# Moving a value product of the context ahead of the second scores, and the second half's value products and sums side by side behind them

## The reference

```
x = x + tanh(g_xattn[0]) * L0_attention(layernorm(x), ctx, ctx)        # causal, 16 heads of 32
x = x + tanh(g_ffn[0])   * L0_ffn(layernorm(x), w_gate_up, w_proj)     # weights made ternary in groups of 64
x = x + tanh(g_xattn[1]) * L1_attention(layernorm(x), ctx, ...)        # projections, normed q and k, softmax, output projection
x = x + tanh(g_ffn[1])   * L1_ffn(layernorm(x), w_gv, w_out)           # ternary weights, 8-bit activations
```

## Time and profile before

| what | before |
|---|---|
| median of 3 runs | 1074.51 us (1073.95 to 1074.6) |
| the profiled execution's own time | 1073.95 us |
| its span, first to last instruction | 1072.2 us |
| TensorE busy | 1046.0 us, 98% |
| VectorE, ScalarE, GpSimd busy | 833.3, 585.6, 119.2 us |
| granted clock of TensorE, mean | 1.000 |
| the chain that ended last, by engine | TensorE 81%, VectorE 11%, ScalarE 2% |

### The profile page before, as it was taken

One profiled execution on the slowest core, in us unless ns is written; L12 is line 12 of the kernel. 1 busy time (PEld: TensorE's weight loads), 2 busy tenths in 40 slices (PEclk: granted clock), 3 DMA queues, 4 the chain that ended last, 5 costly groups with the idle time before them and its releaser, 6 DMA issues.

```text
span 1072.2 us, 24339 instructions
## 1 busy us (share of the span) xinstructions
PE 1046.0 (98%) x9770; PEld 616.8 (58%) x9770; DVE 833.3 (78%) x1440; ACT 585.6 (55%) x893; POOL 119.2 (11%) x212
## 2 busy tenths in 40 slices
PE   8999999999999999999999999999999999999998
PEld 3555555555777777777777664444444444444444
DVE  4988888878777675675766487798898989888987
ACT  4766667677343332333333357638585857573633
POOL 1101001010000000000000212221111111110110
PEclk9999999999999999999999999999999999999999
DMA  9575554552231130330311031214343434331223
GB/s 361 171 256 180 186 186 137 183 157 72 111 80 50 40 80 2 78 79 21 80 40 40 20 106 48 65 40 89 80 90 79 84 85 88 78 66 46 41 59 80
DMA packets 121199, 102.77 MB, mean 96 GB/s; under 512 B 94720, under 2 KB 95232, under 8 KB 120832
## 3 DMA queue, kind: packets, MB, share of 16 engines
q1 hardware_dynamic: 121088, 101.21, 34.6%
HBM read 65.54 MB, written 12.58 MB: 73 GB/s over the span
## 4 chain that ended last, share of the span: by engine, by line
PE 81%; DVE 11%; issue 4%; ACT 2%; DMA 1%; POOL 0%; SPq 0%; DVEq 0%; ACTq 0%; POOLq 0%
PE bank L705 10%; PE bank L704 10%; PE bank L792 10%; PE bank L810 9%; PE bank L669 9%; PE bank L918 6%; PE bank L936 4%; PE bank L906 4%; PE bank L891 2%; PE bank L869 2%; DVE ARENA L1799 2%; PE bank L549 2%; PE bank L574 2%; PE bank L622 2%; PE bank L634 2%
## 5 line engine op out<-in xcount | busy, mean ns | idle before, releaser
L704 PE MATMUL bank<-ARENA,W 128*128 128x256 f16 x1024 | 227.3, 273 | 0.7 <-issue 0.7
L705 PE MATMUL bank<-ARENA,W 128*128 128x256 f16 x1024 | 227.3, 273 | 0.0
L1106 ACT ACTIVATE ARENA<-ARENA 128x512 f16<-128x512 f32 (+1 forms) x96 | 66.8, 707 | 136.9 <-DVE ARENA L1754 132.8
L792 PE MATMUL bank<-W,ARENA 128*128 128x512 bf16 x512 | 120.8, 379 | 0.0
L810 PE MATMUL bank<-ARENA 128*128 128x512 f32 x256 | 118.5, 603 | 2.3 <-DVE ARENA L1841 1.9
L918 PE MATMUL bank<-W,ARENA 128*128 128x512 bf16 x512 | 117.8, 379 | 2.8 <-DVE W L1915 1.7
L669 PE MATMUL bank<-ARENA 128*128 128x512 f32 x256 | 117.9, 603 | 1.1 <-DMA ARENA<-in_wkv 0.8
L704 PEld LDWEIGHTS bank<-ARENA,W 128*128 128x128 bf16 x1024 | 100.2, 98 | 19.3 <-issue 1.3
L705 PEld LDWEIGHTS bank<-ARENA,W 128*128 128x128 bf16 x1024 | 100.2, 98 | 17.9
L2218 POOL TENSOR_TENSOR ARENA<-ARENA 128x2 f32<-128x2 f32 (+1 forms) x72 | 51.4, 714 | 481.4 <-DVE ARENA L1528 247.8
L1754 DVE SCALAR_TENSOR_TENSOR ARENA<-bank,ARENA 128x512 f32<-128x512 f32 x64 | 48.0, 750 | 66.2 <-PE bank L705 63.0
(11 more groups left out here) (190 smaller groups left out, 1743.1 us busy)
## 6 DMA issues: line engine op xcount, KB each, us to landing
W<-in_w SPq DMA_DIRECT2D x48, 512.0 KB, 4.1
ARENA<-in_w SPq DMA_DIRECT2D x24, 512.0 KB, 3.6
kv_store<-ARENA SPq DMA_DIRECT2D x32, 256.0 KB, 4.4
W<-kv_store SPq DMA_DIRECT2D x15, 512.0 KB, 4.5
ARENA<-in_ctxT SPq DMA_DIRECT2D x8, 512.0 KB, 3.8
X<-in_x SPq DMA_DIRECT2D x8, 512.0 KB, 6.6
ARENA<-in_ctx SPq DMA_DIRECT2D x8, 512.0 KB, 6.1
out<-X SPq DMA_DIRECT2D x15, 256.0 KB, 2.2
```

The costliest lines, as they stand in the source:

```text
L704: pe.matmul(bank[:, i * S:(i + 1) * S], W0[:, at:at + P], xt_half(b, 0)[:, k, :], start=(k == 0), stop=False)
L705: mm = pe.matmul(bank[:, i * S:(i + 1) * S], W0[:, at:at + P], xt_half(b, 1)[:, k, :], start=False, stop=(k == KD - 1))
L792: mm = pe.matmul(banks[6 + t], hx(q, what)[:, i * S + t * P:i * S + (t + 1) * P], W0[:, UP_AT + m * D:UP_AT + (m + 1) * D], start=(m == 0 ...
L1106: return act.activation(to, src, ACT.Copy)
```

## The change

In turns 2 to 7 TensorE's order around the second scores changes from: `a_scores(b, 0)`, `a_project(b, 2)`, `a_weigh(e, 1)`, `a_scores(b, 1)`, `a_sum(e, 1)`, `a_project(b, 3)`, `a_group_sum(b, 1)` to: `a_scores(b, 0)`, `a_project(b, 2)`, `a_project(b, 3)`, `a_scores(b, 1)`, `a_weigh(e, 1)`, `a_sum(e, 1)`, `a_group_sum(b, 1)`. ScalarE's copies follow: `a_projected(b, 3)` moves from behind `a_signs(f, 0)` to ahead of `a_weighed(e, 1)`. Turns 1 and 8 keep their order, and so do VectorE, GpSimd and SyncE. No instruction is added or taken away.

```diff
@@ -732,7 +732,10 @@
                 a_scores(b, 0)
                 if end:
                     a_project(turn, b, 2)
-                    a_weigh(turn, e, 1)
+                    if front:
+                        a_project(turn, b, 3)
+                    else:
+                        a_weigh(turn, e, 1)
                 else:
                     a_project(turn, b, 3, (0, 1))
                 a_scores(b, 1)
@@ -740,10 +743,10 @@
                     a_project(turn, b, 3, (2, 3))
                 if not front:
                     b_turn_first()
+                if end and front:
+                    a_weigh(turn, e, 1)
                 if end:
                     a_sum(turn, e, 1)
-                if end and front:
-                    a_project(turn, b, 3)
                 a_group_sum(turn, b, 1)
                 a_max_turn(turn, b, 0)
                 if end:
@@ -1186,13 +1189,15 @@
                     a_abs_sum(b, 0)
                 a_projected(b, 2)
                 if end:
+                    if front:
+                        a_projected(b, 3)
                     a_weighed(e, 1)
                     if not front:
                         b_turn_first()
                     a_summed(e, 1)
                 if front and end:
                     a_signs(f, 0)
-                if front:
+                if front and not end:
                     a_projected(b, 3)
                 a_group_mean(b, 1)
                 a_probs(b, 0)
```

## The result

The changed kernel takes 1079.34 us (median of 6 runs, 1079.0 to 1080.34), the kernel before 1074.47 (6 runs, 1073.62 to 1076.35): 4.87 us more, ratio 1.0045 with a 95% interval of 1.0032 to 1.0058. The forecast was 1079.6 us. The profiled execution of the changed kernel took 1080.34 us, 0.9 to 1.3 us more than its other runs; where that comes from stands at the end.

A forecast was written before the change was run, and what follows sets the result against it. TensorE, busy 98% of the span, was taken as the bound. Five turns x 1.02 = 5.1 us on the profiled 1073.95 gives 1079.05; with 0.56 for the median of the runs, 1079.6 us, range 1077.7 to 1081.6.

The forecast's parts named there:

- The saved joints: TensorE, turns 2 to 7: like-shaped blocks side by side shorten each turn by 0.23 us if nothing waits.
- ScalarE's step: ScalarE's two sign passes now delay the group mean, so TensorE's second group sum starts 1.02 us later each turn.
- The wait 0.7 to 0.9: Sign in the later profile: TensorE's second group sum idles 0.7 to 0.9 us for ScalarE's group mean, five times.
- Turn 2: TensorE already waits there for VectorE's reciprocals, so the change was taken to cost nothing, between -0.2 and +1.0 us.
- Transfers: SyncE's loads of values and w0 go about 4.4 and 3.3 us later, w1 behind the values, at no cost.
- VectorE's step: VectorE's reduction of the second scores and row statistics come later, so the probabilities start 0.27 us late, inside ScalarE's delay.
- case 2: Rival: only VectorE is late, five turns x 0.27 = 1.4 us, 1075.9 us, no difference; chance 0.07.
- the two delays don't add: At TensorE's second group sum, VectorE's delay (start at 130.35) lies inside ScalarE's (131.10).
- The gain: TensorE's six turns, each 0.23 us shorter from fewer shape changes: 1.4 us in all if nothing had to wait.

The follow-up runs named there:

- the old kernel with late signs: Kernel before, TensorE's order untouched, with only ScalarE's a_signs(f,0) moved behind the copy of the second value product: 1082.74 us, ratio 1.0077.
- both cures: Changed kernel with a_signs(f,0) between the value products' copies and, from turn 3, VectorE's row statistics ahead of the second scores' reduction: 1074.03 us, ratio 0.9998.
- the signs early: Changed kernel with ScalarE's a_signs(f,0) moved between the copies of the two value products: 1078.98 us, ratio 1.0045.
- TensorE's part alone: Changed kernel with TensorE's new order kept but ScalarE's old order restored: 1087.52 us, ratio 1.0118.
- the reciprocals first: Changed kernel with a_signs(f,0) between the value products' copies, and VectorE's reciprocals ahead of the two normalisations: 1080.69 us, ratio 1.0062.

## Why the prediction was right, and which step of it was not

- *The saved joints.* 7.07 for P2 and P3: measured 7.07. W and S 2.74: measured 129.75-127.02 = 2.73. Right.
- *ScalarE's step.* G2 was to start 1.02 us later, against P2: measured 14.30-13.30 = 1.00. The mean was to start 2.18 us after the sums' copy: 132.12-129.95 = 2.17. The wait 0.7 to 0.9: measured 0.75. Right, and the old kernel with late signs confirms the same sum at another size. G2 was to wait five times and waits six; the sixth, in turn 2, follows from the prediction's own sum there and costs nothing.
- *Turn 2.* Nothing, between -0.2 and +1.0: measured -0.18. The five others sum to 5.10 as forecast, so turn 2 is most of the distance from 1079.6 to 1079.34.
- *Transfers.* At no cost, right: every wait that grew is put down to ScalarE or VectorE, and with both cures the values and w1 still leave 4.4 us later (the values 126.03-116.43 = 9.60 us after P2, where it was 121.98-116.78 = 5.20) and the time is that of before. That kernel issues w0 only 0.6 later, so for w0's 3.3 us the word is that no wait of any engine in turns 3 to 7 is put down to a transfer.
- *VectorE's step was mis-sized.* The term read "the probabilities start at 129.22, 0.27 late", and case 2 priced VectorE alone at five times 0.27, 1075.9 us. The 0.27 itself is near what is measured, 131.34-118.98 = 12.36 us after P2 where it was 12.17, so 0.19. But the working of this step stopped at the first place at which TensorE waits. Further on it does list the normalisations, the reciprocals and the additions, and puts the ternary work behind them 2.5 us past 129, at 131.5. It began 134.40-118.98 = 15.42 us after P2, at 132.20 on that clock, 0.7 late: the list left out that the normalisations wait for GpSimd's root (0.69 us), which had run in the 0.94 us of idle time of the earlier trace rows, and it did not ask whether TensorE waits for the reciprocals (0.33 us with the signs early). VectorE alone costs 0.84 us in turn 4 (33.92 against 33.08) and 0.75 to 0.93 in turns 3 to 7, three times the term. The sentence that the two delays don't add was right, and that is why the miss did not show in the forecast: the larger one hid it, with less than 0.3 us to spare, and that much is luck. It showed in the experiment with the signs early, which was expected at 1.001 and came at 1.0045.
- *The gain.* "1.4 us in all if nothing had to wait": even with both cures 0.86 us came back by the two profiles' sums (199.64 against 198.78), since a_turn_sums now waits for the sums' copy, which the prediction did not look at.

## What to carry to other kernels

In this kernel an engine without idle time gained little from a tidier order of its own, while each result that it delivers later moves the copies and passes queued behind it on the others: write down for each engine what now stands between the moved result and the next thing that the bound engine needs. Follow every such queue to its next point of slack, not only to the first wait, since idle time that vanishes may have been hiding a third engine's work. When a cure for the named wait gives nothing, look for a second chain of nearly the same length, and try the cures together before dropping either. And read a variant turn by turn where its turns differ in work: one mean over all of them hid here that two explanations each held in some.

## What the runs showed of the hardware

- **The granted clock fell behind some waits of under 2 us and not behind others of the same length.** In the profiled execution of the changed kernel turn 1, whose order is unchanged, has a wait of 1.88 us for a ScalarE copy (0.87 before), and TensorE runs at a mean granted clock of 0.57 behind it:

```profile
33.00:34.90 1.90, 0.08 (x8) 1.00 0.06 24
34.90:37.00 2.10, 2.04 (x36) 0.57 0.04 8
```

  Turn 2 starts at 49.82 there and at 48.43 before: 1.39 us, wait and clock together, that are no part of the change. The other five runs of that kernel, all with a mean clock of 1.000, are 0.9 to 1.3 us faster. In the kernel with TensorE's part alone six waits of 1.75 us came; behind two the clock fell (0.57 and 0.71 above) and in the turns of the others it stayed at 1.00. The ten kept profiles also share a wait of 1.79 to 1.86 us for VectorE between 700 and 716 us, far from the change. Behind it the clock fell in two of them: eight products (L813) took 5.40 us, where the kernel before has 3.70 (L810, at 701.21). In all, it fell behind 6 of 18 waits of 1.75 to 1.90 us. The executions without a profile fit this: those of one kernel with a mean clock of 0.997 or 0.998 are mostly 1 to 3 us longer than those with 1.000. So small differences are read here from the turns of a profile and not from a median alone.
- **A product of VectorE and an addition of GpSimd held each other up.** In the kernel with the reciprocals first, VectorE's product of two 1024-column operands takes 0.69 us, but 1.72 when it begins 0.10 us after a GpSimd addition of 1.27 us. The Trainium skill (SBUF — State Buffer, SBUF: two separate sides) says that a VectorE operation with two SBUF inputs and a GpSimd operation that reads SBUF share one pair of ports as an exclusive lock, and that the second to start is blocked until the first is done. The trace agrees: 137.32+1.27 = 138.59, and the product ends 0.55 us later, at 139.14, with most of its 0.69 behind the addition. In the kernel before it stands once: a product that begins at 48.19, 0.01 after an addition of 1.27, takes 1.81 us, and again ends 0.55 behind it. Where the product begins first it keeps its 0.69 us and the addition is the longer one: 1.55 us in turn 4 of the signs-early kernel, begun 0.27 after a product. No list of waits names either; the blocked instruction is only shown as long.
- **Blocks of one shape side by side took less of TensorE's time**, and no list of waits shows the difference: with one change of shape fewer a turn, the same instructions from P2 up to G1 took 10.77 us instead of 11.01.
